# Longer rows in the transfers of a two-layer cross-attention kernel: contexts, x, and the scratch of split keys and queries

## What is computed

```python
x = x + _L0_xattn_ref(_layernorm(x), ctx_1024, ctx_1024, ...)   # 16 heads of 16
x = x + _L0_ffn_ref(_layernorm(x), ...)      # router, top 6 of 40 experts, 32 with weights
x = x + _L1_xattn_ref(_layernorm(x), ctx_1024, ctx_1024, ...)   # scores times -0.25
x = x + _L1_ffn_ref(_layernorm(x), ...)      # both operands of each product in blockwise FP4
```

## Time and profile before

| | |
|---|---|
| median of three timed runs | 1077.02 us |
| the profiled execution's own time | 1073.0 us |
| its span, first to last instruction | 1071.4 us |
| mean granted clock of TensorE | 0.949 of full speed |
| busy: TensorE, VectorE, ScalarE, GpSimd | 87%, 65%, 39%, 13% of the span |
| packets on SP's queue | 129378, 85.58 MB |
| issue to landing, medians: context, key store, query store | 3.9, 4.6, 3.8 us |

### The profile page before, as it was taken

One profiled execution on the slowest core, in us unless ns is written; L12 is line 12 of the kernel. 1 busy time (PEld: TensorE's weight loads), 2 busy tenths in 40 slices (PEclk: granted clock), 3 DMA queues, 4 the chain that ended last, 5 costly groups with the idle time before them and its releaser, 6 DMA issues.

```text
span 1071.4 us, 20769 instructions
## 1 busy us (share of the span) xinstructions
PE 932.7 (87%) x7430; PEld 724.8 (68%) x7430; DVE 698.3 (65%) x1518; ACT 414.2 (39%) x970; POOL 136.7 (13%) x129
## 2 busy tenths in 40 slices
PE   2996899999989679999998845799999987898987
PEld 1663687788857349898997734577777765455554
DVE  4445577777735805455554464688888885899995
ACT  1342566666645551111111113366665664112211
POOL 7012000000001430000000004000000001344442
PEclk8998899999986989999999979799999998999999
DMA  9688444455032650202112304544544300000000
GB/s 283 179 219 193 94 89 96 100 100 92 17 105 77 172 166 16 76 16 61 31 42 82 107 14 105 108 89 91 99 92 88 77 3 1 5 9 13 13 13 17
DMA packets 129487, 87.07 MB, mean 81 GB/s; under 512 B 52194, under 2 KB 129122, under 8 KB 129378
## 3 DMA queue, kind: packets, MB, share of 16 engines
q1 hardware_dynamic: 129378, 85.58, 34.3%
HBM read 67.52 MB, written 17.79 MB: 80 GB/s over the span
## 4 chain that ended last, share of the span: by engine, by line
issue 32%; PE 28%; DVE 27%; DMA 7%; SPq 2%; POOL 2%; ACT 1%; POOLq 0%; DVEq 0%; ACTq 0%
PE ps L794 12%; DVE ext L1219 8%; PE ps L801 6%; DMA qscr<-qsp 3%; DVE Pr L1167 2%; DVE Pr L1172 2%; DVE Pr L1170 2%; PE ps L651 2%; DMA wgu<-wgu 1%; PE ps L700 1%; DVE amh L1399 1%; DVE Pr L1421 1%; POOL ksp L492 1%; PE ps L561 1%; DMA Qz<-mT 1%
## 5 line engine op out<-in xcount | busy, mean ns | idle before, releaser
L1219 DVE TENSOR_REDUCE ext<-ps 112x2 f32<-112x750 f32 x256 | 235.3, 932 | 57.0 <-PE ps L623 54.7
L986 ACT ACTIVATE Pr<-ps 125x448 f32<-125x448 f32 x384 | 199.1, 542 | 101.7 <-PE ps L637 88.5
L794 PE MATMUL ps<-xT,wgu 128*128 128x224 f32 x704 | 150.7, 357 | 12.9 <-issue 5.1
L794 PEld LDWEIGHTS ps<-xT,wgu 128*128 128x128 f32 x704 | 133.1, 191 | 23.7 <-issue 13.4
L637 PE MATMUL ps<-Qz,Kp 98*125 98x224 f16 x768 | 131.8, 267 | 16.6 <-DMA Qz<-mT 14.2
L623 PE MATMUL ps<-Kp,Qz 96*112 96x375 f16 x512 | 124.5, 335 | 13.1 <-DMA Qz<-qscr 11.9
L637 PEld LDWEIGHTS ps<-Qz,Kp 98*125 98x125 f16 x768 | 95.8, 139 | 50.0 <-DMA Qz<-mT 18.8
L691 PE MATMUL ps<-wv,ctx 128*125 128x256 f32 x384 | 121.2, 400 | 0.5 <-ACT Vx L992 0.4
L561 PE MATMUL ps<-ctx,wk 128*128 128x375 f32 x256 | 96.8, 527 | 27.5 <-DMA bqk<-bqk 13.3
L1337 DVE TENSOR_TENSOR Pr<-Pr,ps 128x224 f32<-128x224 f32 x88 | 34.2, 388 | 129.9 <-ACT Pr L1057 72.5
L873 PE MATMUL ps<-Pr 128*112 128x352 f32 x256 | 83.8, 472 | 16.9 <-DVE Pr L1421 16.5
(11 more groups left out here) (139 smaller groups left out, 1097.7 us busy)
## 6 DMA issues: line engine op xcount, KB each, us to landing
ctx<-ctxT SPq DMA_DIRECT2D x64, 375.0 KB, 3.9
Kp<-kscr SPq DMA_DIRECT2D x96, 187.5 KB, 4.1
kscr<-ksp SPq DMA_DIRECT2D x32, 375.0 KB, 4.6
wgu<-wgu SPq DMA_DIRECT2D x32, 256.0 KB, 2.8
Qz<-qscr SPq DMA_DIRECT2D x192, 28.0 KB, 4.0
wdn<-wdn SPq DMA_DIRECT2D x32, 128.0 KB, 2.9
qscr<-qsp SPq DMA_DIRECT2D x32, 112.0 KB, 3.8
X<-x_in SPq DMA_DIRECT2D x1, 1792.0 KB, 10.6
```

The lines of the kernel that those rows point to most:

```text
L794: last = mm(ps[:, bank, half_ * CT:(half_ + 1) * CT], wgu_sb[e % NE][:, q, EI * half_:EI * half_ + EI], xT2[:, q, c * CT:(c + 1) * CT], st ...
L986: A(Pr[g % 2][0:KC, j, GI * t:GI * t + GI, :].rearrange("r h q -> r (h q)"), ps[0:KC, 4 + k % 2, 0:GI * S], ACT.Exp, scale=scale).then_inc ...
L1219: V.tensor_reduce(ext[0:S, 2 * p:2 * p + 2], ps[0:S, 2 * (p % 2):2 * (p % 2) + 2, 0:M], AX_X, red).then_inc(row_maximum_taken, 1)
```

## The change

No engine gets an instruction more or less, and none is moved. Data lie differently in HBM and in two SBUF buffers, so that rows of transfers are longer:

| transfer | rows before | rows after |
|---|---|---|
| context (64 loads) | 256 of 1500 B | 128 of 3000 B |
| key store (32) | 512 of 750 B | 256 of 1500 B |
| query store (32) | 512 of 224 B | 256 of 448 B |
| x (once) | 1792 of 1024 B | 112 of 16384 B |
| key loads (96), query loads (192) | 256 of 750 B, 128 of 224 B | the same, every second row of the scratch |

The contexts and x are laid out so on the host, before the run.

```diff
-        kscr = nc.dram_tensor("kscr", (B, 2, D, M), F16, kind="Internal").ap()
-        qscr = nc.dram_tensor("qscr", (B, 2, D, S), F16, kind="Internal").ap()
+        kscr = nc.dram_tensor("kscr", (B, C2, 128, 2, M), F16, kind="Internal").ap()
+        qscr = nc.dram_tensor("qscr", (B, C2, 128, 2, S), F16, kind="Internal").ap()
...
-        ksp = [sb(f"ksp{p}", [128, 2, C2, M], F16) for p in (0, 1)]
-        qsp = [sb(f"qsp{p}", [128, 2, C2, S], F16) for p in (0, 1)]
+        ksp = [sb(f"ksp{p}", [128, C2, 2, M], F16) for p in (0, 1)]
+        qsp = [sb(f"qsp{p}", [128, C2, 2, S], F16) for p in (0, 1)]
...
-                sp.dma_start(ctx_sb[par][:, :, :],
-                             ctxT[bass.ds(b, 1)].rearrange("b (c p) m -> p (b c) m", p=128)).then_inc(ctx_loaded[par], 16)
+                sp.dma_start(ctx_sb[par][:, :, :].rearrange("p c m -> p (c m)"),
+                             ctxT[bass.ds(b, 1)].rearrange("b p n -> p (b n)")).then_inc(ctx_loaded[par], 16)
...
-            sp.dma_start(X[:, :].rearrange("q (b d) -> q b d", b=B), x.rearrange("b q d -> q b d")).then_inc(x_loaded, 16)
+            sp.dma_start(X[:, :], x).then_inc(x_loaded, 16)
...
-                sp.dma_start(kscr[bass.ds(b, 1)].rearrange("b s (c p) m -> p (b s c) m", p=128),
-                             ksp[par][:, :, :, :].rearrange("p s c m -> p (s c) m")).then_inc(split_stored[par], 16)
+                sp.dma_start(kscr[bass.ds(b, 1)].rearrange("b c p s m -> p (b c) (s m)"),
+                             ksp[par][:, :, :, :].rearrange("p c s m -> p c (s m)")).then_inc(split_stored[par], 16)
...
-                        kd = kscr[b, kslot(s)].rearrange("(p r) m -> r p m", r=32)
+                        kd = kscr[b, :, :, kslot(s)].rearrange("c (p r) m -> r (c p) m", r=32)
...
-                            qd = qscr[b, qslot(s)].rearrange("(p a r) m -> a r p m", a=2, r=HD)[a]
+                            qd = qscr[b, :, :, qslot(s)].rearrange("c (p a r) m -> a r (c p) m", a=2, r=HD)[a]
...
-                    nc.gpsimd.tensor_tensor(ksp[par][:, 1, :, :], kfull[par], ksp[par][:, 0, :, :],
+                    nc.gpsimd.tensor_tensor(ksp[par][:, :, 1, :], kfull[par], ksp[par][:, :, 0, :],
...
-    args = [give("x_in", g["x"]), give("ctxT", g["ctx_1024"].transpose(0, 2, 1)), attn,
+    args = [give("x_in", g["x"].transpose(1, 0, 2).reshape(S, B * D)), give("ctxT", by_half(g["ctx_1024"].transpose(0, 2, 1))), attn,
```

More of the change, by code:

```diff
@@ L345, in store_queries @@
                     sp.wait_ge(ready, n)
-                sp.dma_start(qscr[bass.ds(b, 1)].rearrange("b s (c p) m -> p (b s c) m", p=128),
-                             qsp[par][:, :, :, :].rearrange("p s c m -> p (s c) m")).then_inc(split_stored[par], 16)
+                sp.dma_start(qscr[bass.ds(b, 1)].rearrange("b c p s m -> p (b c) (s m)"),
+                             qsp[par][:, :, :, :].rearrange("p c s m -> p c (s m)")).then_inc(split_stored[par], 16)
             for l in (0, 1):
                 def load_values_ctx(b, par):
-                    sp.dma_start(ctx_sb[par][:, :, :],
-                                 ctxT[b].rearrange("(c p) m -> p c m", p=128)).then_inc(values_ctx_loaded[par], 16)
+                    sp.dma_start(ctx_sb[par][:, :, :].rearrange("p c m -> p (c m)"), ctxT[b]).then_inc(
+                        values_ctx_loaded[par], 16)
                 def load_kq(b):
@@ L934, in keys_high @@
                 for m in range(C2):
-                    last = A(ksp[par][:, 0, m, :], ps[:, 4 * l + 2 * par + m, 0:M], ACT.Identity,
+                    last = A(ksp[par][:, m, 0, :], ps[:, 4 * l + 2 * par + m, 0:M], ACT.Identity,
                              bias=bqk[l][:, 2 + m:3 + m])
@@ L955, in queries_high @@
                     for m in range(C2):
-                        last = A(qsp[par][:, 0, m, :], ps[:, 4 + par, m * S:(m + 1) * S], ACT.Identity,
+                        last = A(qsp[par][:, m, 0, :], ps[:, 4 + par, m * S:(m + 1) * S], ACT.Identity,
                                  bias=bqk[l][:, m:m + 1])
@@ L1184, in split_low @@
                         for m in range(C2):
-                            last = V.scalar_tensor_tensor(ksp[par][:, 1, m, :], ps[:, 2 * par + m, 0:M],
-                                                          bqk[l][:, 2 + m:3 + m], ksp[par][:, 0, m, :],
+                            last = V.scalar_tensor_tensor(ksp[par][:, m, 1, :], ps[:, 2 * par + m, 0:M],
+                                                          bqk[l][:, 2 + m:3 + m], ksp[par][:, m, 0, :],
                                                           ALU.add, ALU.subtract)
@@ L1190, in split_low @@
                     for m in range(C2):
-                        last = V.scalar_tensor_tensor(qsp[par][:, 1, m, :], ps[:, 4 + par, m * S:(m + 1) * S],
-                                                      bqk[l][:, m:m + 1], qsp[par][:, 0, m, :], ALU.add, ALU.subtract)
+                        last = V.scalar_tensor_tensor(qsp[par][:, m, 1, :], ps[:, 4 + par, m * S:(m + 1) * S],
+                                                      bqk[l][:, m:m + 1], qsp[par][:, m, 0, :], ALU.add, ALU.subtract)
                     last.then_inc(queries_low_ready, 1)
@@ L1473, in give, with by_half @@
         return nc.dram_tensor(name, a.shape, mybir.dt.from_np(a.dtype), kind="ExternalInput").ap()
+    def by_half(a):
+        return a.reshape(B, C2, 128, M).transpose(0, 2, 1, 3).reshape(B, 128, C2 * M)
     g = {k: np.asarray(v) for k, v in inputs.items()}
```

## The result

The changed kernel takes **1064.4 us** (median of 4 runs, 1062.4 to 1065.3) beside 1076.8 us for the kernel before (4 runs, 1071.9 to 1079.1): ratio 0.988, 95% interval 0.985 to 0.991, a gain of 12.4 us. Two later sets beside other experiments gave 1063.6 against 1072.9 (0.991, 0.989 to 0.994) and 1063.0 against 1073.6 (0.990, 0.987 to 0.993). The gain is thus 9 to 12 us, about twice the 5.0 of the forecast, and 1064.4 lies under the range.

The account below looks back on a forecast made before the run. Store landings in two-buffer loops and x were taken to bound the stages around attention. Terms 0.76 + 2.0 + 0.3 + 1.0 + 0.8 + 0.15 = 5.0 us, from 1077.0 to 1072.0 us; range 1066.0 to 1077.0.

Parts of the forecast that it names:

- loads from the scratch did not slow down: Rival at both attention starts: key loads, 4.1 us, take up to twice that; 1088 us; chance 0.07 including slower x.
- Layer 0's loop: Projection of layer 0: one landing per two batches is on the path, 0.29 us shorter, 7 times, 2.0 us.
- The queries of layer 1: Query-store landings in layer 1: 0.115 us goes on 7 of 14 waits, forecast as 0.8 us.
- Is there more than rows in a landing?: Lone key against query store: 0.62 us of the difference is row time, 0.5 goes with bytes, which stay; nothing added.
- The price of a row: All transfers: each row saved gives its DMA engine 7.2 ns, while bytes cost what they did.
- Keys of layer 1: Key store and context save 0.17 us a landing, on 6 of 12 waits, 1.0 us.
- The bound from above, 8.6: Keys of layer 1: landings fall from the 4.6 us median to 3.16 alone, at most 6 x 1.4 = 8.6 us.
- Start of layer 0's attention: Batch 2 is loaded once the last stores have landed and the maxima follow: one landing, 0.3 us.
- x: Load of x at the start, on the path before VectorE's statistics and TensorE's first queries: gains 0.76 us.
- The doubt about ports: Load of x: 112 partitions may limit its SBUF ports, so it may keep 6.9 us; sum 0.76 less.
- Contention goes too: Rival in layer 0's loop, keys of layer 1 and x: contention falls too, 11 us gained, 1066 us; chance 0.12.
- Landings are latency: Rival for store landings: saved row time is lost, only x is left, 0 to 3 us, about 1076; chance 0.23.

Follow-up runs that it names:

- 768 B places: Kernel before with the same 512 key rows of 750 B, each beginning at a multiple of 768 B in the scratch; 1060.9 us beside 1078.5 (0.985).
- Queries alone: Kernel before with only the queries' scratch laid out anew, 256 rows of 448 B a store; 1068.4 us beside 1071.7 (0.996).
- x alone: Kernel before with only x laid out anew, 112 rows of 16384 B; 1068.4 us beside 1071.7 (0.997).
- padded rows, as many as before: Kernel before with the queries' scratch padded, 512 rows of 256 B a store; single run 1076.4 us beside 1078.5.
- keys alone: Kernel before with only the keys' scratch laid out anew, 256 rows of 1500 B a store; 1062.7 us beside 1071.7 (0.991).
- contexts alone: Kernel before with only the contexts laid out anew, 128 rows of 3000 B; 1071.5 us beside 1071.7 (1.000).
- the whole change without x: Changed kernel with x kept at 1792 rows of 1024 B; 1061.1 us beside 1072.9 for the kernel before (0.988).

## Why the prediction was wrong in size

- **Where** was right: the gain is in the loops with two buffers, the packets fell as counted, and loads from the scratch did not slow down.
- **Layer 0's loop** came out in size (2.0 forecast, 2.3 in the pair of profiles), but that is luck, at least in part. Key rows at 768 B places, with not one row fewer, gave 3.6 there (47.29 us against 50.87), nearly all of the 3.7 that TensorE's bound leaves. Queries alone were worth 7 x 0.115 = 0.8 by the forecast and gave nothing (50.94); but x alone, which leaves this stage as it was, shows 0.9 (49.93), so single profiles tell no finer than that. The queries of layer 1 (0.8 forecast, 0.9) are luck in part: padded rows, as many as before, give 0.6 of it.
- **The step that failed** is "Is there more than rows in a landing? ... So I add nothing for it." The price of a row was right as engine time: 256 fewer packets take a lone store from 29% of 4 us on 16 engines to 26%. But a row also has a price in the landing beyond its time on the engine, if it begins off a boundary, and this term was put at nothing. I put the 0.5 us between query and key store down to bytes; the kernel with 768 B places lands a key store 0.5 us sooner with the same bytes and rows. Places of rows were never asked about, though rows of 750 B back to back begin at every multiple of 2 B.
- **Keys of layer 1**: forecast 1.0, measured 4.5. The bound from above, 8.6, held it; the value came from row times alone. The landing that 6 of 12 waits hang on fell by 0.7 at the median of this stage's 16 stores (4.0 to 3.4) and by 0.8 at that of all 32, so 6 x 0.7 to 0.8 = 4 to 5 us is close. This is the sign that the prediction had named for a wrong size, landings in the mixed stages that fall by more than 0.3. Why 0.7 in the mixed stage and 0.4 alone was not separated.
- **Start of layer 0's attention**: forecast 0.3, 1.5 in the pair of profiles. The pair overstates it: x alone, which leaves this part as it was, has 0.8 there too, keys alone 0.6 and the 768 B places 0.9. That the landings of the key stores did it is likely and was not shown.
- **x**: forecast 0.76, nothing. The chain of waits went through x because VectorE's statistics wait for it; but behind them L1130 was held by GpSimd's memset, which the chain cannot name, since no semaphore is involved. An instruction ten times as long as the same line elsewhere (1.76 us against 0.17) was there to be read. The Trainium skill, SBUF — State Buffer, Who interferes with whom, names VectorE's `tensor_scalar` as one that can contend with GpSimd for a port held for a whole instruction. The 1.76, 0.66 and 0.17 us agree. The doubt about ports does not follow from the section of the Trainium skill that the prediction names for it, SBUF — State Buffer, Door 1: by its table partitions 0 to 111 reach all 16 ports, as 0 to 127 do. No run here shows why x moves fewer bytes a second than the weights. Whether long rows help x stays open: x alone was 3.2 us faster, the whole change without x 2.5 us faster than with it. x landed in 10.6 to 14.9 us with 1024 B rows (16 profiles) and in 11.7 to 12.6 with 16 KB (4).
- **The rivals.** "Contention goes too" named 1066 us with a chance of 0.12. Its sum was nearest, its cause was not: contexts alone gave 0.2 us. "Landings are latency" was right that most of a landing is not row time, and wrong that the rest cannot change.

## What to carry to other kernels

A store's landing is more than its packets' time: look at the time from the last bytes to the landing, and let rows in scratch begin at multiples of 32 B or more before making them longer (8 and 16 B were not tried with rows of this length); a changed pitch cost three lines here, the scratch, its store and its loads. When one stage gets faster, ask which step of another chain stands in its order of work (here the router's product), for it is the next bound. On a path, compare each instruction's duration with the same line elsewhere in the trace: an unusually long one is a wait that the chain does not show.

## What the runs showed of the hardware

- A lone key store of 512 rows of 750 B landed 3.3 to 3.5 us after its issue with rows at multiples of 2 or 4 B (7 profiles), and 2.8 us with the same rows at multiples of 256 B (2 profiles), at the same speed and engine time. The time from its last bytes to the landing was 0.7 to 1.2 us and 0.4 us.
- VectorE's `tensor_scalar` on 112x16 numbers takes 0.17 us alone and up to 1.76 beside GpSimd's memset; the memset itself takes half as long with half as many numbers of twice the size (5.09 us against 10.09).
- One transfer of x took 10.6 to 14.9 us from issue to landing in different executions with nothing of it changed.
